# A constant tile multiplied on TensorE ahead of three waits of a cross-attention and mixture-of-experts kernel

## What is computed

```python
q = layernorm(x) @ Wq.T;  k = ctx @ Wk.T;  v = ctx @ Wv.T
sim = einsum('bqd,bkd->bqk', q, k)
sim = (sim - mean(sim)) * rsqrt(var(sim) + 1e-5)       # over each batch's whole matrix
x = x + (softmax(sim) @ v) @ Wo.T
h = layernorm(x)
probs = softmax(h @ gate_w + gate_b)
cw = probs where among the top 2 of 8, else 0
x = x + swiglu(h @ sw1 + sb1) @ sw2 + sb2 + sum_e cw[e] * (swiglu(h @ rw1[e] + rb1[e]) @ rw2[e] + rb2[e])
```

## Time and profile before

| | |
|---|---|
| median of 3 runs | 155.4 us (154.41 to 155.75) |
| the profiled execution's own time | 152.72 us |
| its span, first to last instruction | 150.7 us |
| mean granted TensorE clock | 0.966 of 2.4 GHz |
| TensorE, VectorE, ScalarE, GpSimd busy | 88%, 72%, 47%, 16% |

### The profile page before, as it was taken

How to read it: one execution, slowest core, us unless ns; L and a number is a source line. 1 busy time by engine, 2 the same in 40 slices (tenths; PEclk the granted TensorE clock), 3 DMA queues, 4 the chain that set the end, 5 groups by cost and what they waited for, 6 DMA issues and landing times.

```text
span 150.7 us, 2018 instructions
## 1 busy us (share of the span) xinstructions
PE 132.1 (88%) x603; PEld 96.5 (64%) x603; DVE 108.1 (72%) x337; ACT 70.6 (47%) x132; POOL 23.7 (16%) x41
## 2 busy tenths in 40 slices
PE   0998894498999999499999998899899989999980
PEld 0786681486878766368778775667576656766740
DVE  3676968486886988974966988829986883865641
ACT  2347955666133127973353129962133783313320
POOL 7083366304020001040200000000300000000000
PEclk9999997558999999999999999999999999999999
DMA  4999000000000000009510000049020008720002
GB/s 127 298 340 255 6 0 7 0 0 2 0 0 4 0 0 2 0 23 325 213 66 8 0 0 0 5 148 382 33 70 0 0 4 229 327 70 7 0 0 72
DMA packets 8493, 11.38 MB, mean 76 GB/s; under 512 B 1265, under 2 KB 6922, under 8 KB 8098
## 3 DMA queue, kind: packets, MB, share of 16 engines
q1 hardware_dynamic: 7906, 11.02, 21.9%
q10 hardware_dynamic: 576, 0.23, 0.6%
HBM read 10.15 MB, written 1.10 MB: 75 GB/s over the span
## 4 chain that ended last, share of the span: by engine, by line
issue 49%; PE 28%; POOL 8%; DVE 6%; ACT 3%; DMA 2%; POOLq 1%; DVEq 0%
PE bank L836 24%; POOL ln_rstd L358 3%; POOL row_powers L349 2%; DMA ctx_sb<-in_ctx_dram 2%; POOL sim_r L364 2%; ACT prob L437 2%; POOL w_rest L371 1%; PE bank L852 1%; POOLq L49 1%; PE bank L844 1%; DVE xn L601 1%; PE bank L995 1%; DVE act L754 0%; DVE silu L746 0%; ACT silu L485 0%
## 5 line engine op out<-in xcount | busy, mean ns | idle before, releaser
L485 ACT ACTIVATE silu<-bank,b_cols 128x512 f32<-128x512 f32 (+1 forms) x37 | 24.9, 676 | 47.2 <-PE bank L836 43.7
L836 PE MATMUL bank<-x_head,w_head 128*128 128x512 f32 x72 | 39.7, 552 | 0.0
L836 PE MATMUL bank<-act,w_sb 128*128 128x512 f32 (+1 forms) x74 | 36.4, 580 | 0.0
L836 PE MATMUL bank<-x_head,w_rest 128*128 128x512 f32 x72 | 28.9, 401 | 0.0
L754 DVE SCALAR_TENSOR_TENSOR act<-bank,b_cols,silu 128x512 f32<-128x512 f32 (+1 forms) x37 | 27.2, 736 | 2.2 <-ACT silu L485 1.4
L836 PE MATMUL bank<-x_rest,w_head 128*128 128x512 f32 x72 | 28.8, 399 | 0.0
L746 DVE TENSOR_TENSOR silu<-silu,cw_all 128x512 f32<-128x512 f32 (+1 forms) x25 | 16.7, 667 | 13.3 <-DMA cw_all<-cw_dram 7.2
L836 PEld LDWEIGHTS bank<-x_head,w_head 128*128 128x128 f32 x72 | 14.0, 195 | 7.6 <-issue 4.6
L836 PEld LDWEIGHTS bank<-x_rest,w_head 128*128 128x128 f32 x72 | 14.1, 195 | 6.7 <-issue 5.2
L836 PEld LDWEIGHTS bank<-act,w_sb 128*128 128x128 f32 x74 | 13.7, 188 | 3.6 <-issue 1.0
L836 PEld LDWEIGHTS bank<-x_head,w_rest 128*128 128x128 f32 x72 | 13.9, 193 | 3.3
(11 more groups left out here) (113 smaller groups left out, 186.1 us busy)
## 6 DMA issues: line engine op xcount, KB each, us to landing
cw_all<-cw_dram SPq DMA_DIRECT2D x3, 1024.0 KB, 6.9
cw_all<-cw_dram SPq DMA_DIRECT2D x6, 256.0 KB, 3.5
cw_all<-cw_dram SPq DMA_DIRECT2D x3, 512.0 KB, 4.9
x_sb<-in_x_dram SPq DMA_DIRECT2D x4, 256.0 KB, 4.0
w_sb<-in_L_ffn_rw_dram SPq DMA_DIRECT2D x1, 1024.0 KB, 7.2
ctx_sb<-in_ctx_dram SPq DMA_DIRECT2D x4, 192.0 KB, 4.1
out_dram<-x SPq DMA_DIRECT2D x3, 256.0 KB, 2.1
w_sb<-in_L_ffn_rw_dram SPq DMA_DIRECT2D x1, 512.0 KB, 7.2
```

The costliest lines, as they stand in the source:

```text
L485: scalar.activation(silu[:, k, cols], HID[(2 * n) % 3][:, cols], ACT.Silu, bias=b1_cols[:, 0, e:e + 1]).then_inc(silu_sb, 1)
L836: return pe.matmul(dst, lhs, rhs, start=start, stop=stop, skip_group_check=True)
```

## The change

A tile `blank` of 128 x 128 ones is written by VectorE as its first operation. TensorE multiplies it by itself, with 128 columns each time and into a PSUM bank that nobody reads: 30 times at the very start of its program (into bank 7), ahead of the wait for the first transfer; 12 times behind `project_u(2)` and ahead of `transpose_x2(0)` (into bank 0, after the wait for `setup_sb` that so far stood behind the router); and 24 times between `transpose_x2(0)` and `router(0)`. The old wait behind the router stays too. Nothing else changes.

```diff
+        blank = sb("blank", [P, P], F32R)
...
+            dve.memset(blank[:, :].bitcast(F32), 1.0).then_inc(blank_ready, 1)
             dve.wait_ge(ident_ready, 1)
...
+            def keep_clock(dst, count):
+                for _ in range(count):
+                    mm(dst[:, 0:P], blank[:, :], blank[:, :])
+
+            pe.wait_ge(blank_ready, 1)
+            keep_clock(LATE, 30)
             pe.wait_ge(ident_ready, 1)
             transpose_ctx(0)
...
             project_u(2)
+            pe.wait_ge(setup_sb, 3)
+            keep_clock(bank[0], 12)
             transpose_x2(0)
+            keep_clock(bank[0], 24)
             router(0)
             pe.wait_ge(setup_sb, 3)
```

More of the change, by code:

```diff
@@ L147, in xattn_moe_kernel @@
         ident_ready, consts_ready, pool_order = sem("ident_ready"), sem("consts_ready"), sem("pool_order")
-        pick_clear = sem("pick_clear")
+        pick_clear, blank_ready = sem("pick_clear"), sem("blank_ready")
         w_heads, w_rests = sem("w_heads"), sem("w_rests")
```

## The result

The changed kernel takes 156.22 us in the median of 20 runs (155.06 to 158.97); beside it the kernel before took 154.50 in 20 runs (152.36 to 155.82). The ratio is 1.0175, with a 95% interval of 1.0131 to 1.0219: slower by 1.7 us, against a forecast of 1.8. The medians here are taken over all runs of a kernel, while the ratios leave out slow runs, those more than 1.5% above the fastest of their kernel, and so are not the quotients of the medians beside them.

The account below looks back on a forecast made before the run. TensorE, busy 88% of the span, was taken as the bound, behind an early chain over several engines with little slack. Start +2.8 and middle -1.0 gave +1.8 on the 155.4 median: 157.2 us, range 154.8 to 160.2.

Parts of the forecast that it names:

- The price of a blank: Each blank costs its weight load, 0.211 us at 1.2 GHz and 0.112 at 2.4, with streaming taken as covered.
- The third rival: At the start, blanks cost 0.107 us even at 1.2 GHz and fit the transfer wait; 153.7 us, chance 0.12.
- The opening: Thirty blanks ahead of the first transfer overrun its wait and delay the average `sim_avg`; +2.8 us.
- the path through VectorE: Opening: fixed VectorE work from the Wk-Wq product to the maxima, passing its delay on to `sim_avg`.
- up 6.7 us after the first blank: Opening: the clock rises at 7.7, all thirty and the first transposes are slow; average 2.4 us late.
- not brought up at all: Opening: blanks do not raise the clock, the same slow stretch starts from 7.3; everything shifts by 3.2 us.
- the router's stretch: Around the router, the clock rose only after TensorE had worked 6.7 us; taken as the nearer model for the blanks.
- the three cases: Opening: clock up 3.7 us after the first blank, 6.7 us after, or not through blanks; +1.0, +2.4 or +3.2 us.
- The middle: Twelve and 24 blanks around the row transposes keep the router at full clock; first spread 1.0 us earlier.
- The condition: Around the router, the 12 and 24 are covered by waits only if the clock stays up.
- The later fall: Clock falls at new waits for `cw_cols` and `cw_t` before 36.4; +1.8 to +3.3 us on the forecast, chance 0.10.
- The two terms: Thirty blanks at the start, +2.8 us, and the 12 and 24 around the row transposes, -1.0 us.

Follow-up runs that it names:

- the run with 16 columns: Changed kernel with the thirty start blanks streaming 16 columns instead of 128, and the 12 and 24 left out; 156.80 us in one run.
- the fourteen: Changed kernel with 14 instead of 30 blanks at the start, the 12 and 24 kept; 153.25 us, ratio 1.004 to the kernel before.
- the six long ones: Changed kernel with six 512-column blanks replacing the thirty at the start, 12 and 24 kept; 153.63 us, ratio 0.984. Three later kernels share this start.
- the last experiment: Kernel before plus only eight 512-column blanks ahead of the eighth spread of expert weights; 152.32 us against 155.28, ratio 0.990.

## Why the prediction was right, and where it was not

**The price of a blank.** Taken from the router's products, 0.211 at 1.2 GHz and 0.112 at 2.4; measured 0.215 and 0.11. That streaming is covered was an assumption, and the run with 16 columns bears it out. The third rival, a price of about 0.107 at 1.2 GHz too, is out. The page "TensorE: Matmul & The Clock Gate" of the Trainium skill, section "LDWEIGHTS", gives a load's time as its columns over 1.2 GHz, with no term for the granted clock, from which 107 ns for 128 columns is estimated; at 1.2 GHz this trace has twice that.

**The opening.** The start (1.0, measured 1.05), the end of the thirty (7.3, measured 7.5) and the path through VectorE held. Taken was +2.8, the middle between "up 6.7 us after the first blank" and "not brought up at all"; the profile gave 3.24, the second, so this term was 0.4 short there. In medians the thirty cost 2.4 (157.51 against 155.09) and 2.7 (154.70 against 152.02). The argument that short products behind full loads resemble the router's stretch, through which the clock stayed low, is borne out by the fourteen and the thirty, which brought the clock up no sooner, and by the six long ones, which did so in three of four profiles. That the clock rises a fixed time after the first product, as the three cases take it, is not: with no blanks at the start, the stretch from the first transpose to `sim_avg` varied by 1.3 us among five profiles.

**The middle.** -1.0 forecast, 1.0 measured between `sim_avg` and the first spread, in the parts that were named: 0.81 in the router (30.30 - 28.32 = 1.98 from its first product to the logits before, 32.67 - 31.50 = 1.17 after), and the rest because the weight transposes no longer queue behind hidden layers. VectorE's chain from the logits to `cw_cols` did not shorten (5.56 us before, 5.57 after). The condition, twelve products ahead of the transposes, is shown by the run without them, in its profile and, as far as their clocks tell, in seven of its eight runs.

**The later fall.** It was a rival at 0.10, and that was too little: with 12 and 24 alone 4 of 12 runs lost 2 us or more, and the profile among them shows the fall at the wait for `cw_cols`. The evidence brought against it, that the wait ahead of 62.50 left the clock up, came from one execution, and by the last experiment it did not hold in most executions of that same kernel. In the changed kernel's profile the fall is at that old wait, not at the new one, and costs 1.64 us that the sum does not have.

**How far the sum was luck.** The two terms the sum was made of have the right causes and nearly the right sizes. That 1.8 was forecast and 1.7 measured is closer than they deserve: from profile to profile the change cost 3.2. The forecast was set on the median, 2.7 us above the profiled execution, and carried that difference along unexplained; over 20 runs it is 1.8, and the later fall, which the kernel before usually seems to pay too and its profile does not, is a likely part of it. Nor do the parts add up in the medians: the thirty alone give +2.4, the 12 and 24 alone -3.3, together -0.9 and not +1.7. By the ratios they give +1.4% and -0.8%, which with their intervals is not against the 1.75% of the whole.

**What stays open.** Why the six long products alone, or the 12 and 24 alone, also thin out the times near 155, with the wait ahead of the eighth spread untouched. They move TensorE's whole course by about a microsecond, and it may be that the fall depends on when a wait of 2 us comes; no run here varied only that. Of the nine profiles in which the eighth spread waits its 2 us unfilled, three have a fall behind it.

## What to carry to other kernels

Work put in to keep a clock up is paid in the clock that is there: count it at the slow rate, and against the wait it is to fill, before it is put ahead of anything real. At the start, products as long as the real ones did here what short ones did not; in the middle, twelve and 24 short ones mostly sufficed. Look for the wait that a faster stretch opens: here TensorE then waited for `cw_cols`, and in some executions the clock fell there. When a kernel's median lies 2% over its profiled execution, find that difference first; here it was worth more than the change, and the kernel with all these waits filled takes 150.9 us where the one before takes 155.

## What the runs showed of the hardware

- 6.5 us of weight loads with 128 or 16 columns streamed behind each left TensorE at 1.2 GHz; behind six products of 512 columns from 1.45 to 4.2 it was at 2.4 GHz by 5.7 in three profiles of four, and in the fourth by about 7.2.
- Products that each load 128 columns of this type are spaced 0.215 us at 1.2 GHz, with 16 or with 128 columns streamed, and 0.11 at 2.4, with 16 (the router) or with 128 (the 24).
- The clock row prints 1.00 from the start of the span, through a stretch in which the instructions run at half speed.
- A wait of 2.0 us in otherwise dense work was followed by a fall in the changed kernel's profile, which cost 1.64 us, and by none in the one before; with the wait filled the median of the kernel before went from 155.3 to 152.3.
